# A two-layer network on one core: the DRAM scratch of Q, K and V laid out like the operand rows

## The reference

```
x = layernorm(x + linear_attention(x))      # layer 0: norms of Q and K over the tokens, D x D matrices
x = layernorm(x + mixture_of_experts(x))    # 8 experts, softmax gate with a threshold
qkv = x @ Wqkv.T                            # layer 1: 16 heads, 16 channels each
scores = einsum('bnhd,bngd->bnhg', q, k) / 8        # for each token, head against head
out = einsum('bnhg,bngd->bnhd', softmax(scores), v) @ Wproj.T + bproj
x = layernorm(x + out)
x = layernorm(x + mixture_of_depths(x))     # the top 75% of the tokens by a router get gelu(x @ W)
```

## Time and profile before

| | us |
|---|---|
| median of 3 runs | 1611.36 (1608.79 to 1613.42) |
| the profiled execution | 1609.18 |
| its span, first to last instruction | 1607.4 |
| TensorE matmul busy | 1255.6 (78%) |
| VectorE busy | 958.1 (60%) |
| ScalarE busy | 669.8 (42%) |
| GpSimd busy | 601.5 (37%) |
| packets of the SyncE queue | 90170, 79.93 MB, 25.6% of 16 DMA engines |

### The profile page before, as it was taken

One profiled execution on the slowest core, in us unless ns is written; L12 is line 12 of the kernel. 1 busy time (PEld: TensorE's weight loads), 2 busy tenths in 40 slices (PEclk: granted clock), 3 DMA queues, 4 the chain that ended last, 5 costly groups with the idle time before them and its releaser, 6 DMA issues. The chain is left out here.

```text
span 1607.4 us, 33289 instructions
## 1 busy us (share of the span) xinstructions
PE 1255.6 (78%) x12232; PEld 791.7 (49%) x12232; DVE 958.1 (60%) x2185; ACT 669.8 (42%) x1164; POOL 601.5 (37%) x889
## 2 busy tenths in 40 slices
PE   7689869976998868986898869988789777774452
PEld 4454546543664546553565537545465435531441
DVE  2434666685656747485556756477466866475535
ACT  3322552355432752344623662336523553253423
POOL 2133271344522543335613545324713435243212
PEclk9789977998879977989789887999779886797556
DMA  4000442018120370207320180205520080208220
GB/s 149 14 5 16 102 63 54 15 40 147 16 67 7 95 99 10 59 14 141 47 67 8 66 127 3 66 8 121 72 54 1 27 149 11 54 3 159 24 54 27
DMA packets 92918, 90.78 MB, mean 56 GB/s; under 512 B 7031, under 2 KB 81721, under 8 KB 92474
## 3 DMA queue, kind: packets, MB, share of 16 engines
q1 hardware_dynamic: 90170, 79.93, 25.6%
q0 software_dynamic: 2560, 8.39, 1.5%
HBM read 46.35 MB, written 41.94 MB: 55 GB/s over the span
## 5 line engine op out<-in xcount | busy, mean ns | idle before, releaser
L1430 PE MATMUL bank<-we,at 128*128 128x512 f16 x1536 | 397.3, 423 | 98.0 <-DVE x L1143 49.1
L1430 PEld LDWEIGHTS bank<-we,at 128*128 128x128 f16 x1536 | 161.2, 107 | 317.1 <-issue 126.1
L513 POOL TENSOR_TENSOR part<-part 128x512 f32<-128x512 f32 x64 | 81.2, 1269 | 353.3 <-ACTq L792 353.2
L651 ACT ACTIVATE part<-bank,wexp 128x256 f32<-128x256 f32 x256 | 104.3, 470 | 202.0 <-PE bank L1430 156.9
L768 ACT ACTIVATE x<-x,nm,rs 128x256 f32<-128x256 f32 x192 | 104.4, 593 | 132.5 <-POOL nm L501 132.0
L1143 DVE SCALAR_TENSOR_TENSOR x<-bank,wexp,x 128x256 f32<-128x256 f32 x256 | 122.7, 479 | 56.8 <-PE bank L1430 46.8
L1430 PE MATMUL bank<-bt,wqkv 128*128 128x512 f16 x576 | 138.8, 382 | 20.9 <-DVE stage L985 18.3
L985 DVE TENSOR_TENSOR stage<-bank,stage 128x512 f16<-128x512 f32 x128 | 86.3, 686 | 102.7 <-ACT stage L651 102.7
L651 ACT ACTIVATE blockdiag<-shared,const 128x2048 f16<-128x2048 f16 x64 | 122.7, 1990 | 36.4 <-POOL shared L545 35.6
L651 ACT ACTIVATE stage<-bank 128x512 f16<-128x512 f32 x128 | 75.2, 596 | 125.5 <-PE bank L1430 82.1
L494 POOL TENSOR_SCALAR nm<-mv 128x2 f32<-128x2 f32 x128 | 29.7, 232 | 259.7 <-DVE mv L1020 254.8
(11 more groups left out here) (175 smaller groups left out, 2209.9 us busy)
## 6 DMA issues: line engine op xcount, KB each, us to landing
scratch_qkv<-stage SPq DMA_DIRECT2D x48, 512.0 KB, 3.4
ct<-scratch_qkv SPq DMA_DIRECT2D x128, 128.0 KB, 5.9
x_in<-in_x_dram SPq DMA_DIRECT2D x32, 256.0 KB, 2.7
keys<-scratch_qkv SPq DMA_DIRECT2D x64, 128.0 KB, 10.9
scratch_o<-stage SPq DMA_DIRECT2D x64, 128.0 KB, 3.1
bt<-scratch_o SPq DMA_DIRECT2D x16, 512.0 KB, 3.7
out_dram<-x POOLq DMA_DIRECT2D x32, 256.0 KB, 2.6
blockdiag<-in_expert_w_dram SPq DMA_DIRECT2D x1, 2048.0 KB
```

The source lines that it names most:

```text
L513: pool.tensor_tensor(part[:, 0:2, :], part[:, 0:2, :], part[:, 2:4, :], ALU.add)\
L651: return act.activation(dst, src, ACT.Copy, scale=scale)
L1430: ins = pe.matmul(dst, lhs, rhs, start=(n == 0), stop=(n == len(terms) - 1))
```

## The change

The scratch keeps its size. Its order becomes, for each of Q, K, V, (token residue r, channel d, head h, 256 elements) for Q and K, and (r, head, channel, 256 elements) for V: the same order as the partitions and rows of `ct` and `keys`. A store of a tile becomes eight DMAs, one for each head of the tile, of 16 partitions x 8 runs of 512 bytes. Each load becomes one DMA of 128 rows of 8 KB that lie one behind the other in DRAM. The counts of the semaphores follow (`STORES` = 128 a tile instead of 16 on `stored`; 16 instead of 128 a batch on `q_loaded`, `k_loaded`, `v_loaded`). The order on every engine stays.

```diff
-        q_src, k_src, v_src = [scratch_qkv[D * n:D * (n + 1)].rearrange("(h d) (r n) -> h d r n", d=DH, r=T)
-                               for n in range(3)]
+        head_rows = scratch_qkv.rearrange("(m r d x) (y n) -> m r d (x y) n", m=3, r=T, x=2, n=2 * P)
+        q_src, k_src, v_src = [head_rows[m].rearrange("r d h n -> (r d) (h n)") for m in range(3)]
...
+        STORES = 16 * H // 2
...
-                sp.dma_start(scratch_qkv[P * ft:P * (ft + 1)], stage[:, ft % 2, :]).then_inc(stored[ft % 2], 16)
+                for h in range(H // 2):
+                    head = H // 2 * (ft % 2) + h
+                    rows = head_rows[ft // 2, :, :, head, :] if ft < 4 else head_rows[2, :, head, :, :]
+                    sp.dma_start(rows.rearrange("r d n -> d r n"),
+                                 stage[DH * h:DH * (h + 1), ft % 2, :].rearrange("p (r n) -> p r n", r=T))\
+                        .then_inc(stored[ft % 2], 16)
...
+            def rows_stored(b, m):
+                for s in range(2):
+                    sp.wait_ge(stored[s], STORES * (3 * b + m + 1))
+                    sp.sem_inc(waits_held, 1)
...
             def b_loadq(b):
...
-                for r in range(T):
-                    sp.dma_start(compact_rows(r), q_src[:, :, r, :].rearrange("h d n -> d h n")).then_inc(q_loaded, 16)
+                sp.dma_start(ct[:, :, :, :].rearrange("p k l n -> p (k l n)"), q_src).then_inc(q_loaded, 16)
...
-                for r in range(T):
-                    sp.dma_start(keys[DH * r:DH * (r + 1), :, :],
-                                 k_src[:, :, r, :].rearrange("h d n -> d h n")).then_inc(k_loaded, 16)
+                sp.dma_start(keys[:, :, :].rearrange("p h n -> p (h n)"), k_src).then_inc(k_loaded, 16)
...
-                for r in range(T):
-                    sp.dma_start(compact_rows(r), v_src[:, :, r, :]).then_inc(v_loaded, 16)
+                sp.dma_start(ct[:, :, :, :].rearrange("p k l n -> p (k l n)"), v_src).then_inc(v_loaded, 16)
...
-                    act.wait_ge(stored[(k // 2) % 2], 48 * b + 16 * (k // 4))
+                    act.wait_ge(stored[(k // 2) % 2], STORES * (3 * b + k // 4))
```

More of the change, by code:

```diff
@@ L388, in b_f @@
                 sp.sem_inc(waits_held, 1)
-                sp.dma_start(scratch_qkv[P * ft:P * (ft + 1)], stage[:, ft % 2, :]).then_inc(stored[ft % 2], 16)
-            def compact_rows(r):
-                return ct[DH * r:DH * (r + 1), :, :, :].rearrange("p k l n -> p (k l n)")\
-                    .rearrange("p (h n) -> p h n", h=H)
+                for h in range(H // 2):
[4 more added lines that the diff above has]
+                        .then_inc(stored[ft % 2], 16)
@@ L395, in b_loadq @@
+            def rows_stored(b, m):
+                for s in range(2):
+                    sp.wait_ge(stored[s], STORES * (3 * b + m + 1))
+                    sp.sem_inc(waits_held, 1)
             def b_loadq(b):
-                for s in range(2):
-                    sp.wait_ge(stored[s], 48 * b + 16)
-                    sp.sem_inc(waits_held, 1)
+                rows_stored(b, 0)
                 if later(b):
                     sp.wait_ge(ff_full, 4 * b)
-                for r in range(T):
-                    sp.dma_start(compact_rows(r), q_src[:, :, r, :].rearrange("h d n -> d h n")).then_inc(q_loaded, 16)
+                sp.dma_start(ct[:, :, :, :].rearrange("p k l n -> p (k l n)"), q_src).then_inc(q_loaded, 16)
@@ L404, in b_loadk @@
             def b_loadk(b):
-                for s in range(2):
-                    sp.wait_ge(stored[s], 48 * b + 32)
-                    sp.sem_inc(waits_held, 1)
-                for r in range(T):
-                    sp.dma_start(keys[DH * r:DH * (r + 1), :, :],
-                                 k_src[:, :, r, :].rearrange("h d n -> d h n")).then_inc(k_loaded, 16)
+                rows_stored(b, 1)
+                sp.dma_start(keys[:, :, :].rearrange("p h n -> p (h n)"), k_src).then_inc(k_loaded, 16)
@@ L413, in b_loadv @@
             def b_loadv(b):
-                for s in range(2):
-                    sp.wait_ge(stored[s], 48 * b + 48)
-                    sp.sem_inc(waits_held, 1)
+                rows_stored(b, 2)
                 sp.wait_ge(q_turned, 2 * b + 2)
-                for r in range(T):
-                    sp.dma_start(compact_rows(r), v_src[:, :, r, :]).then_inc(v_loaded, 16)
+                sp.dma_start(ct[:, :, :, :].rearrange("p k l n -> p (k l n)"), v_src).then_inc(v_loaded, 16)
             def b_loado(b):
@@ L461, in _ @@
             for s in stored:
-                sp.wait_ge(s, 48 * NB)
+                sp.wait_ge(s, STORES * 3 * NB)
             sp.wait_ge(o_stored, 16 * T * NB)
@@ L539, in b_turnq @@
                 if hf == 0:
-                    pool.wait_ge(q_loaded, 16 * T * (b + 1))
+                    pool.wait_ge(q_loaded, 16 * (b + 1))
                     pool.sem_inc(waits_held, 1)
@@ L549, in b_turnv @@
                 if hf == 0:
-                    pool.wait_ge(v_loaded, 16 * T * (b + 1))
+                    pool.wait_ge(v_loaded, 16 * (b + 1))
                     pool.sem_inc(waits_held, 1)
@@ L1592, in b_s @@
                 if q == 0:
-                    pe.wait_ge(k_loaded, 16 * T * (b + 1))
+                    pe.wait_ge(k_loaded, 16 * (b + 1))
                 pe.wait_ge(q_spread[q // 2], b + 1)
```

## The result

The changed kernel takes 1615.27 us (median of 20 runs, 1605.73 to 1628.82), the kernel before on the same chips 1611.63 us (20 runs). The ratio is 1.0036, 95% interval 1.0019 to 1.0054: a little slower, where 1592 us was forecast. The profiled execution took 1615.10 us, its span is 1613.3 at a mean granted clock of 0.838 (before: 1607.4 at 0.837).

The account below looks back on a forecast made before the run. TensorE is fullest at 78% of the span, the rest waits. Batches 1 to 5 -5, batch 0 -3, batch 6 -5, batch 7 -6.5: -19.5 us from 1609.2, 1589.7; median 2.2 above, 1592 us, range 1571 to 1612.

Parts of the forecast that it names:

- the sum for the turns with a jump: Batches 1 to 5: tail +2.3 us, gap on "issue" -3.3, net -1.0 us a turn, -5 us in all.
- V's earlier arrival: In turns with a jump, V landing sooner gives nothing more, since TensorE is nearly without a gap behind the jump.
- The gap on "issue": Code fetch behind the loop's jump, slowed by 512-byte reads: 3.3 of 10 us to go, bounds 0 and 5.
- Rival (a): The gap behind the jump is the fetch's own latency, so 5 x 3.3 us is missing: 1608, no change; chance 0.18.
- The trains: Eight stores a tile at 0.42 us each land later, delaying F10's eviction and the tail of every turn by 2.3 us.
- rival (b): SyncE needs 0.77 us a store, slipping F10 and the Q load 2.5 us more in all 8 batches: 1620; chance 0.12.
- The waits of F6: ScalarE's F4, F6 and F8 wait for stores, 1 to 2 us late, absorbed by normalisations except in batch 7.
- The net of a turn: Turns with a jump, batches 1 to 5: 2.3 - 3.3 = -1.0 us each.
- Batch 0: VectorE's 3.39 us wait goes, the tail takes 2.3 back, a spread free of GpSimd's copies gives 2: -3 us.
- Batches 6 and 7: Batch 6: shorter spread and ScalarE's 3.73 us wait gone, -5 us. Batch 7: Q 2.6 us earlier, -6.5 us.
- The loads: Q, K, V loads as one DMA of 8 KB rows: 4.5 us to landing, bounds 3.7 and 8.2 + 2.
- rival (d): 8 KB rows load no faster than 512-byte ones, Q lands 0.9 us later than now: 1615 and more; chance 0.02.

Follow-up runs that it names:

- e1: Changed kernel with GpSimd's turning of V made to wait until VectorE has finished its spread of Q: 1586.28 us, ratio 0.9845 to the kernel before.
- e2: Changed kernel with GpSimd held ("the hold") ahead of the subtractions and V's turn until VectorE has spread Q: 1575.47 us, ratio 0.9787.
- e3: Kernel before with K's loads held until GpSimd has turned the first half of Q: 1652.06 us, ratio 1.0259.
- e5: Changed kernel with a third buffer slot for the Q, K, V tiles, stores still trains of eight: 1607.40 us, ratio 0.9983.
- e7: Changed kernel with GpSimd held until VectorE has spread Q, and each V tile stored by one DMA: 1572.62 us, ratio 0.9785.
- e9: Changed kernel with GpSimd held until VectorE has spread Q, a third tile buffer, and each V tile stored by one DMA: 1566.72 us, ratio 0.9722.
- e6: Kernel before with GpSimd held until VectorE has finished its spread of Q: 1610.56 us, ratio 0.9987.

## Why the prediction was wrong

**The step that failed** is in the sum for the turns with a jump: "V's earlier arrival gives nothing more here, since TensorE is nearly without a gap behind the jump." I had V's arrival as something that could only help or be idle. It costs: GpSimd acts on it at once, 10 us earlier, and takes from VectorE what they share while VectorE spreads Q, which the same change had also moved up. By the turns, after against e1, it costs 6.4 to 7.2 us in each of batches 1 to 4, 26.8 us together. Batch 5 is 7.3 us longer than in e1 too, but by the other collision, of the gate's steps with GpSimd's copy of an earlier Q; the sum had no term for that one either. Together that is 34 us over batches 1 to 5 (938.8 against 904.8), and with batch 0 (185.2 against 177.8 in e2) 41 us; the medians of after and e2 are 39.8 us apart. The sizes stood in my rows: 8.80 us for the spread beside GpSimd's copy in batch 6 against 6.31. I used them for a gain in batch 0 and did not ask which work of GpSimd the spread would meet in its new place.

**The gap on "issue".** Allowed 3.3 of 10 us, bounds 0 and 5; TensorE's fell to 3.3 to 5.0, by 5.6 us in the mean, and VectorE's to 2.6 to 3.6, by 6.7, outside the bounds. Rival (a), that it is the fetch's own latency, fails; e3 shows by itself that K's reads make it longer. My bound came from counting the fetch packets' times; that they also stand in line would explain the rest, but no row shows it. What V's writes add is small: TensorE's gap is 2.9 to 4.2 us in e3, where there are none of the new kind.

**The trains.** SyncE needs 3.6 to 5.5 us for eight, once 7.0 (an issue 0.43 us in the median, 0.42 taken), F10 starts at F1 + 20.4 to 21.7 instead of 18.2 to 19.7, and the tail ends 1.4 to 3.1 us later in batches 1 to 4, 2.3 in the mean: the +2.3 stands, and rival (b) with 0.77 us an issue did not happen. ScalarE behind batch 3, F6 and F10:

```profile
750.25 0.60 ACT L647 ACTIVATE stage<-bank 128x512 f16<-128x512 f32 x1 [4.33 <-DMA scratch_qkv<-stage]
...
758.68 0.60 ACT L647 ACTIVATE stage<-bank 128x512 f16<-128x512 f32 x1 [1.40 <-DMA scratch_qkv<-stage]
```

The waits of F6 (3.6 to 4.3 us in batches 1 to 5, 1 to 2 taken) and F8 are the most of ScalarE's 56.8 us. In batches 1 to 4 they were absorbed, as forecast: F7's store goes out at F1 + 15.1 to 15.6, before at 14.4 to 16.0, and F10 starts when it has landed. In batch 5 F8 was 3.2 us late, and F11 and the gate behind it met GpSimd's copy of Q.

**The net of a turn.** In e2, without the collision, the tail is 3.5 us later in the mean of the five turns and TensorE's gap 5.5 us shorter, so TensorE starts again 2.0 us earlier, for the 1.0 forecast. The turns are 3.8 us shorter than those before (905.2 against 924.4, over five). The other 1.8 us had no term: 1.4 lie between TensorE's new start and its first transpose, where the stop of 1.07 us between the expert tiles is gone, and 0.4 behind it.

**Batch 0** was to gain 3, of which 2 by a spread free of GpSimd's copies. It lost 3.1: the tail, 3.8 us later instead of 2.3, took back the whole wait of 3.39 us, and the spread ran beside the subtractions and the V copy together, 14.4 us instead of 12.3. With the hold it is 6.7, and the batch gains 4.3.

**Batches 6 and 7** came right, -5.9 for -5 and -7.2 for -6.5. Batch 6 has no subtractions, and its spread is through (F1 + 37.3) just before GpSimd copies V (37.4). The last batch after:

```profile
1485.96 3.62 POOL L541 COPY prob<-ct 128x2048 f16<-128x2048 f16 x1 [10.69 <-DMA ct<-scratch_qkv]
...
1493.17 15.27 ACT L647 ACTIVATE blockdiag<-shared,const 128x2048 f16<-128x2048 f16 x8 [10.20 <-POOL shared L541]
...
1512.67 1.12 PE L1605 MATMUL bank<-const,prob 128*128 128x128 f32 x4 [8.23 <-POOL prob L554]
```

Q is 21.9 us behind F1 (1464.1) instead of 23.6, 1.7 earlier for the 2.6 forecast, and the first transpose 48.6 instead of 53.8, 5.2 earlier for the 6.5; 2 us more came behind it.

**The loads.** 5.5 us to landing, K's 7.2, for the 4.5 taken, within the bounds; rival (d), reads no faster than before, did not happen: between 1134 and 1138 us, when a load of Q runs beside a train, the queues move 294 GB/s. But what made the old loads slow is open. The prediction laid 128 GB/s against 364 on the runs of 512 bytes and took it as a test of the 512 B that it cites; the two rows differ in a second way, since each old load fills 16 partitions and each of `bt`'s all 128. The change altered both at once, and no run parts them. The window's columns: us, busy time (instructions) of the five engines, granted clock, DMA share, GB/s.

```profile
1134.00:1138.00 4.00, 4.00 (x63) 2.35 (x62) 2.14 (x8) 2.14 (x3) 0.00 (x0) 0.50 0.87 294
```

In sum: of the 25.4 us between the forecast (-19.5) and the outcome (+5.9 over the cuts), 19.4 lie in batches 1 to 5, 6.1 in batch 0 and 1.5 ahead of the first F1, where the change does nothing, less the 1.6 that batches 6 and 7 gained beyond the forecast.

## What to carry to other kernels

When an edit makes data arrive earlier, write down which engine acts on it at once and what its neighbour will be doing at that moment: here 10 us of earlier V turned a gain of 4 us a turn into a loss of 3, and one added wait turned it back. Where their operands lie in SBUF, VectorE and GpSimd are to be scheduled against each other as if they were one resource, and a busy time that grows at an unchanged count of instructions is the sign to look for. When an edit shows nothing, look for the stage that sets the period (here the first transpose) before giving the edit up.

## What the runs showed of the hardware

- An engine that jumps back to a loop's start stands 2.4 to 6.7 us on "issue" where K's old loads (16 partitions each, in 512-byte runs) are out of the way (after, e1 to e3, e5, e7 to e9), and 8.8 to 10.5 us where they are in the queues, 1 MB in all (before, e6).
- GpSimd copies of 3.6 to 3.8 us stretched VectorE's instructions on SBUF to about the copy's length, however short they are alone: 0.23 to 3.30 us, 0.20 to 3.50 us and 0.74 to 4.17 us.
- The mean granted clock rose with the hold, from 0.838 to 0.854, though TensorE had the same work in less time. Behind a stop of 6.90 us the same 24 matmuls ran at a granted clock of 0.78 and took 6.78 us; behind one of 1.07 us they ran at 1.00 and took 5.35.
